# Adding each expert block straight into the output instead of summing the two expert results at the end

## The reference, cut to what matters

```python
xn = _layernorm(x, axis=-1)                       # x is 4096 x 256, float32
x = x + attention_and_ffn(xn) + experts(xn)

# experts(xf): 8 experts, 2 per token, F = 816
scores = softmax(xf @ gate_w.T + gate_b)
top_w, top_idx = top_k(scores, 2)
top_w = top_w / (top_w.sum(-1, keepdims=True) + 1e-20)
comb = zeros((N, E)).at[arange(N)[:, None], top_idx].add(top_w)
for e in range(E):
    h = silu((xf @ gp_w[e].T + gp_b[e]) * (xf @ up_w[e].T + up_b[e]))
    y += comb[:, e:e+1] * (h @ down_w[e].T + down_b[e])
```

## Time and profile before

| | us |
|---|---|
| median of 3 runs (lowest to highest) | 1273.86 (1269.78 to 1274.48) |
| the profiled execution | 1273.59 |
| its span, first to last instruction | 1271.7 |
| PE busy | 1119.9 (88%) |
| DVE busy | 880.4 (69%) |
| ACT busy | 852.1 (67%) |
| POOL busy | 633.3 (50%) |

### The profile page before, as it was taken

How to read it: one execution, slowest core, us unless ns; L and a number is a source line. 1 busy time by engine, 2 the same in 40 slices (tenths; PEclk the granted TensorE clock), 3 DMA queues, 4 the chain that set the end, 5 groups by cost and what they waited for, 6 DMA issues and landing times.

```text
span 1271.7 us, 29969 instructions
## 1 busy us (share of the span) xinstructions
PE 1119.9 (88%) x9148; PEld 1038.1 (82%) x9148; DVE 880.4 (69%) x2032; ACT 852.1 (67%) x1994; POOL 633.3 (50%) x912
## 2 busy tenths in 40 slices
PE   3978898989897979888999999999999989999950
PEld 3966686868686868777889999999999989999950
DVE  7467564747465655656678888888888888788825
ACT  2355766758585857586478887777787878887830
POOL 6003543233232314052167777777677767777750
PEclk9997898989898999999889999999999999999985
DMA  8870011010101010031241111114411240125119
GB/s 293 271 223 22 34 35 51 21 45 25 41 29 37 33 37 33 26 130 35 103 145 39 33 33 33 33 60 175 162 60 33 86 144 28 41 86 197 44 52 345
DMA packets 66258, 106.72 MB, mean 84 GB/s; under 512 B 7277, under 2 KB 57966, under 8 KB 64560
## 3 DMA queue, kind: packets, MB, share of 16 engines
q1 hardware_dynamic: 58624, 86.55, 20.9%
q0 software_dynamic: 7600, 19.74, 4.4%
HBM read 138.52 MB, written 37.50 MB: 138 GB/s over the span
## 4 chain that ended last, share of the span: by engine, by line
PE 36%; ACT 26%; DVE 19%; issue 13%; DMA 2%; SPq 1%; DVEq 1%; ACTq 1%; POOL 0%; POOLq 0%
PE bank L1198 9%; PE bank L1199 8%; PE bank L1200 8%; ACT hf L786 5%; DVE gu_s L1117 5%; ACT sm L689 4%; ACT gu_s L797 3%; ACT dw_s L804 3%; ACT gs L779 3%; DVE hf L1137 3%; PE bank L1295 3%; DVE gu_s L1124 3%; PE bank L1323 2%; DVE ys L1153 2%; PE bank L1285 2%
## 5 line engine op out<-in xcount | busy, mean ns | idle before, releaser
L1198 PE MATMUL bank<-xt_h,gu_s 128*128 128x256 f32 (+1 forms) x1014 | 294.8, 291 | 16.1 <-DVE hf L1137 11.3
L1199 PE MATMUL bank<-xt_l,gu_s 128*128 128x256 f32 (+1 forms) x1014 | 288.7, 285 | 0.0
L1200 PE MATMUL bank<-xt_h,gu_s 128*128 128x256 f32 (+1 forms) x1014 | 288.1, 284 | 0.0
L616 POOL TENSOR_TENSOR ht<-hf,ht 128x256 fp32r<-128x256 f32 (+1 forms) x273 | 240.2, 892 | 48.1 <-ACT ht L790 47.0
L1124 DVE TENSOR_TENSOR gu_s<-raw_gu,gu_s 128x512 fp32r<-128x512 f32 (+1 forms) x273 | 196.9, 744 | 64.0 <-ACT gu_s L797 63.9
L1198 PEld LDWEIGHTS bank<-xt_h,gu_s 128*128 128x128 f32 (+1 forms) x1014 | 193.5, 191 | 23.0 <-issue 19.8
L1200 PEld LDWEIGHTS bank<-xt_h,gu_s 128*128 128x128 f32 (+1 forms) x1014 | 193.5, 191 | 0.0
L1199 PEld LDWEIGHTS bank<-xt_l,gu_s 128*128 128x128 f32 (+1 forms) x1014 | 193.3, 191 | 0.0
L786 ACT ACTIVATE hf<-hf 128x256 f32<-128x256 f32 (+1 forms) x273 | 113.5, 416 | 77.0 <-DVE hf L1137 72.3
L1198 PE MATMUL bank<-dw_s,ht 128*128 128x256 f32 x546 | 154.8, 284 | 2.2 <-issue 2.2
L1200 PE MATMUL bank<-dw_s,ht 128*128 128x256 f32 x546 | 154.8, 283 | 0.0
(11 more groups left out here) (176 smaller groups left out, 2748.1 us busy)
## 6 DMA issues: line engine op xcount, KB each, us to landing
raw_gu<-in_gu_dram SPq DMA_DIRECT2D x39, 1648.0 KB
raw_dw<-in_dw_dram SPq DMA_DIRECT2D x39, 896.0 KB
xs_dram<-zrec SPq DMA_DIRECT2D x6, 1677.0 KB, 14.6
xr<-xs_dram SPq DMA_DIRECT2D x39, 258.0 KB, 2.7
yg<-y_dram SPq DMA_DIRECT2D x16, 512.0 KB, 8.3
xwin<-xn_dram SPq DMA_DIRECT2D x8, 640.0 KB, 4.8
xg<-in_x_dram SPq DMA_DIRECT2D x8, 512.0 KB, 6.3
xn_dram<-xg SPq DMA_DIRECT2D x8, 512.0 KB, 7.9
```

The source lines that it names most:

```text
L616: nc.gpsimd.tensor_tensor(ht[0:m, p, 1, c, :], hf[0:m, ring(c), :], ht[0:m, p, 0, c, :].bitcast(F32), ALU.subtract).then_inc(h_split, 1)
L1198: nc.tensor.matmul(dst, lhs[0], rhs[0], start=start, stop=False)
L1199: nc.tensor.matmul(dst, lhs[0], rhs[1], start=False, stop=False)
L1200: return nc.tensor.matmul(dst, lhs[1], rhs[0], start=False, stop=stop)
```

## The change

Three things change. The dense sums are stored to `out` by SP as soon as they are ready, seven groups in the dense stage and the last one in the beginning of the expert stage. For each expert block POOL gathers the block's rows of `out` with two indirect DMAs (`rows_so_far`) into `sofar`, which lies in the first four row tiles of `xn`; DVE adds them while it weighs, and the scatter goes to `out`. The last pass (`load_rows`, `add_rows`, the stores) is gone, and so is `y_dram`. POOL waits for all eight stores and clears `sofar` once before its first block.

```diff
@@ SP
+            def store_out(g):
+                sp.dma_start(out_g[ds(g, 1)].rearrange("o p t d -> p (o t) d"), xn[:, ds(g * GT, GT), :]).then_inc(out_stored, 16)
...
                 load_residual(at.g)
+                store_out(at.f)
...
             load_gu(2, 0)
             load_dw(1, 1, False)
+            store_out(NG - 1)
             load_rows_of(2, 0)
...
             sp.wait_ge(y_sent[0], 32 * ((NB + 1) // 2))
             sp.wait_ge(y_sent[1], 32 * (NB // 2))
-            (load_rows, store_out and their loop over the eight groups)
@@ POOL
+            def rows_so_far(b, p):
+                if not isinstance(b, int) or b >= 1:
+                    pool.wait_ge(y_sent[1 - p], (b + p) * 16)
+                if not isinstance(b, int) or b >= 2:
+                    settle(pool)
+                    pool.wait_ge(y_sent[p], (b - p) * 16)
+                pool.wait_ge(y_kept, b * 2 + 2)
+                settle(pool)
+                for t in range(2):
+                    index = dest[:, 2 * p + t:2 * p + t + 1]
+                    nc.gpsimd.indirect_dma_start(sofar[:, p, t, :], None, out, bass.IndirectOffsetOnAxis(index, 0),
+                                                 bounds_check=S - 1, oob_is_err=False).then_inc(sofar_loaded[p], 16)
...
             def body(b, p):
                 for c in range(FCH):
                     h_low(b, p, c)
                     if c == 2:
                         keep_meta(b, p)
+                    if c == FCH - 1 and (not isinstance(b, int) or b >= 1):
+                        rows_so_far(b - 1, 1 - p)
                 for c in range(DV, FCH):
                     dw_low(b, p, c)
                 if not isinstance(b, int) or b >= 1:
                     send(b - 1, 1 - p)
+            pool.wait_ge(out_stored, 16 * NG)
+            nc.gpsimd.memset(xn[:, 0:4, :], 0.0).then_inc(sofar_set, 1)
+            pool.wait_ge(sofar_set, 1)
             blocks_of(pool, body)
+            rows_so_far(NB - 1, (NB - 1) % 2)
             send(NB - 1, (NB - 1) % 2)
@@ DVE, weigh
+                dve.wait_ge(sofar_loaded[p], through(b, p, 32))
                 for t in range(2):
-                    ins = nc.vector.tensor_scalar(ys[:, p, t, :], bank[5 + p][:, t * D:(t + 1) * D], wgt[:, p, t:t + 1], None, ALU.mult)
+                    ins = nc.vector.scalar_tensor_tensor(ys[:, p, t, :], bank[5 + p][:, t * D:(t + 1) * D], wgt[:, p, t:t + 1], sofar[:, p, t, :], ALU.mult, ALU.add)
...
-            (add_rows and its loop)
```

More of the change, by code:

```diff
@@ L20 @@
 GT = 4
-YB = 4
 XB = 4
@@ L137, in program @@
     xs_dram = nc.dram_tensor("xs_dram", (SLOTS, REC), F32, kind="Internal").ap()
-    y_dram = nc.dram_tensor("y_dram", (2 * S, D), F32, kind="Internal").ap()
     with ExitStack() as ctx:
@@ L232, in program @@
         ys = tile("ys", [2, 2, D])
+        sofar = xn[:, 0:4, :].rearrange("p (b t) d -> p b t d", t=2)
         dest = tile("dest", [4], U32)
@@ L235, in program @@
         third.close()
-        fourth, tile = phase()
-        yg = tile("yg", [YB, 2, GT, D])
-        fourth.close()
         const_loaded, small_loaded, zrec_ready, xs_filled, pads_filled = sems("const_loaded small_loaded zrec_ready xs_filled pads_filled")
@@ L266, in program @@
         y_sent = sems("y_sent_0 y_sent_1")
-        yg_loaded = sems("yg_loaded_0 yg_loaded_1 yg_loaded_2 yg_loaded_3")
-        sum_1, sum_2, out_stored = sems("sum_1 sum_2 out_stored")
+        out_stored, sofar_set = sems("out_stored sofar_set")
+        sofar_loaded = sems("sofar_loaded_0 sofar_loaded_1")
         x_g = x.rearrange("(g t p) d -> g p t d", t=GT, p=P)
@@ L490, in _ @@
             sp.wait_ge(y_sent[1], 32 * (NB // 2))
[L492 to L508, removed]
         @block.gpsimd
@@ L521, in _ @@
             pool.wait_ge(zrec_ready, 1)
-            nc.gpsimd.iota(zrec[:, D:D + 1].bitcast(I32), [[0, 1]], base=2 * S, channel_multiplier=1).then_inc(zrec_ready, 1)
+            nc.gpsimd.iota(zrec[:, D:D + 1].bitcast(I32), [[0, 1]], base=S, channel_multiplier=1).then_inc(zrec_ready, 1)
             for n, (_, dst, chunks, width) in enumerate(DENSE):
@@ L622, in send @@
                     index = dest[:, 2 * p + t:2 * p + t + 1]
-                    nc.gpsimd.indirect_dma_start(y_dram, bass.IndirectOffsetOnAxis(index, 0), ys[:, p, t, :], None,
-                                                 bounds_check=2 * S - 1, oob_is_err=False).then_inc(y_sent[p], 16)
+                    nc.gpsimd.indirect_dma_start(out, bass.IndirectOffsetOnAxis(index, 0), ys[:, p, t, :], None,
+                                                 bounds_check=S - 1, oob_is_err=False).then_inc(y_sent[p], 16)
             def body(b, p):
@@ L898, in route_weights @@
                 for k in range(2):
-                    link(nc.vector.tensor_scalar(meta[:, k, :, 0].bitcast(I32), cst[:, C_TOK:C_TOK + NT], float(k * S), None, ALU.add))
+                    link(nc.vector.tensor_copy(meta[:, k, :, 0].bitcast(I32), cst[:, C_TOK:C_TOK + NT]))
             def route_starts(at):
@@ L1180, in _ @@
             weigh(NB - 1, (NB - 1) % 2)
[L1183 to L1191, removed]
         @block.tensor
```

## The result

The changed kernel takes 1378.3 us (median of 4 runs, 1375.84 to 1380.22) against 1272.3 us before (4 runs, 1269.78 to 1274.48): a ratio of 1.083, 95% interval 1.080 to 1.086. It is slower, as forecast, but by 106 us where 24 were forecast, and far above the range. The profiled execution spans 1376.0 us (before 1271.7), so 104.3 us are to be explained.

What follows compares the result with a forecast made beforehand. DMA bound the last pass, PE the expert stage. Added 9 + 1.5 + 48 + 2.7 = 61.2 us, less 37.5 removed, net +23.7 on 1273.59, gave 1298 us; the 8-in-10 range was 1274 to 1326.

Steps and rivals of the forecast that it cites:

- The direction: Whole kernel: slower by net 23.7 us; the chance of slower in all was put at 0.78.
- The stores in the dense stage: Seven 512 KB stores on SP's queue, covered by PE's work: cost 0, about 10 us if the cover were gone.
- The first block: POOL's first h_low waits for the last store and the clearing, delaying DVE and PE: 9 us, bounds 5 and 12.
- the first gather: The gather of block 0 adds one more 1.5 us, outside the 36 steady periods.
- The landing after the second gather: In each block, 2.4 to 2.7 us from the second gather's start; weigh period 16.6 us instead of 15.09.
- Rival C: Slow gathers: 3.5 us landings in all blocks, 1338 us; or 2 us each in nine weight-load blocks, 1316; chance 0.13.
- The loads: Blocks with weight loads: of 8 us excess over 36 periods, 6 absorbed because scatters stand about 1.4 us earlier.
- The removed pass: Last pass, 37.8 us to the span's end, less about 0.3 of closing instructions: gain 37.5 us in full.
- the end: Last two blocks wait for their gathers; the last scatters land at 1236.5 against 1233.87: 2.7 us added.
- what POOL loses in idle time: POOL's extra gather work, 39 x 2.5 us, fits its idle time, being busy 443 of 614 us: cost 0.
- rival A: Gather short and mostly hidden in each block, 0.7 us a block: 1264 us; chance 0.10.
- Rival D: PE's clock falls once in five blocks for some 7 us, costing 14 us: 1312 us; chance 0.05.

Runs made afterwards that it cites:

- experiment 1: Changed kernel without the gathers; DVE weighs by a multiply alone, so the output lacks the dense part in gathered rows: 1250.3 us, ratio 0.979.
- experiment 4: Changed kernel with DVE's one 128x1024 subtraction (dw_low) cut in four of 128x256: 1336.6 us, ratio 1.047.
- Experiment 3: Changed kernel with one more wait on SP, so the gate/up weight load is issued only after POOL's dw_low of the same body: 1342.6 us, ratio 1.052.
- Experiment 2: Changed kernel with the gathers issued by POOL, but DVE neither waits for them nor adds them: 1298.7 us, ratio 1.017.
- experiment 5: Changed kernel with the two gathers moved on POOL from behind the last h_low to behind keep_meta, after its third h_low: 1338.7 us, ratio 1.049.
- e10: Changed kernel weighing block b-2 behind chunk 2 of body b, scatter behind the third h_low, last store awaited at the first gather: 1271.9 us, ratio 0.998.
- e6: Changed kernel without clearing the tile, POOL's wait for the last store moved from before the first block to before the first gather: 1371.6 us, ratio 1.074.
- e9: Changed kernel weighing block b-2 behind chunk 3 of body b, scatter behind the fourth h_low, last store awaited at the first gather: 1286.2 us, ratio 1.011.

## Why the prediction was wrong

**Right.** The direction, and what paces the stage: `weigh` waits for the second gather in every block and PE for the product behind it. The stores in the dense stage were free, as worked out. So was part of the account of the loads: POOL's wait for a slow scatter (15.0 us in 8 waits) is gone in the changed kernel. The first block's +10.3 us for 10.5 is in part luck: counted from the end of the dense stage in each profile, `weigh` 0 is 6.7 us late in experiment 1, without gathers (I took 9), and the first gather adds 2.9 (I took 1.5).

**The landing after the second gather was mis-sized** ("lands after 2.4 (what the second of a quiet pair takes)"). It is 3.6 to 3.7 us from the start of the issue, also 0.9 more than the 2.7 that I allowed at most. I read the scatters' row, whose second issue takes 1.00 us at a place where DVE is past its long operation. A gather issued where I put it begins within that operation, and experiment 4 shows that this alone costs 0.86 us. I had written that DVE "is still at its splits" there and still allowed only 0.3 us. The h_low end was 0.4 us earlier than I took, which gave a part back; net 0.68 us a block, 24.4 us in all. Rival C's first form (3.5 us in every block) had the landing nearly right.

**The loads were mis-sized, and with the wrong sign** ("I count 6 of the 8 us as absorbed"). I looked only at the wait that I knew, for the scatters, and not at where the new gather lies against SP's loads, though rival C says that they "start about 1 us behind the second gather and could overtake it". C gave it 2 us in nine blocks; these nine are 5.3 us longer each (47.6 us), 4.2 of it the wait for the gather. Experiment 3 shows it: 36 us come back by a later load alone; and in experiment 4 eight of the nine go by an issue that ends before the load starts. C's two forms together are what happened, and I had priced each on its own and never their sum: 40 + 18 us above 1298 is 1356, still 22 short.

**The removed pass was worth 34.5 us, not 37.5**, since the program's closing isn't 0.3 us; and the end costs 4.7 us for 2.7, since each of the last gathers also takes longer.

**What no rival had**: POOL's issues cost by themselves. I had put "what POOL loses in idle time" at 0, from its 443 busy us of 614. Experiment 2 puts the period at 16.2 with nothing waiting for the data. In the changed kernel the wait hides this floor (17.28), so the term isn't in the miss, but rival A (1264 us if the gather is hidden) could never have come true in this order of work; experiment 5, built on it, came 64 us above its range. Rival D's clock falls came (mean 0.94 where before it was 0.99): four quiet periods of 18.1 instead of 17.3 make 3 us, and up to some 10 us more lie in the load blocks, behind the idle that the collisions make. The latter is read from the lengths of the periods, and no run tests it apart.

What stays open: in experiment 1 the closing from the last `weigh` takes 10.8 us, and 8.3 to 8.4 in the changed kernel and all the others; and what sets e10's period.

## What to carry to other kernels

When a pass that runs alone at the DMA's rate is turned into one small transfer a block, compare it with the number of blocks times the slack of the engines that issue it and wait for it, and not with bytes: here 2.2 us more in each of 36 periods, and 5.3 on top in nine of them, outweighed 34.5 us of a pass that moved 12.6 MB. Price a new DMA from the operations of the neighbouring engine at its exact place and from the loads that start before its issue ends, in the blocks where there are any. Let what it fetches be wanted a third of a block later, not next.

## What the runs showed of the hardware

- An indirect DMA's issue on POOL takes 1.0 to 1.4 us nearly everywhere, unless it begins while a DVE operation with two inputs of 128x1024 f32 (1.23 us) runs. An issue that began 0.1 to 1.0 us into it ended 0.87 to 0.96 us behind its end, in the changed kernel and in e2, e3, e6 and e9: it took 2.06 us when begun 0.11 us into it, 1.88 at 0.24, 1.57 at 0.6. The 28 of e10 that began 0.1 to 0.2 us before it took 1.07 or 1.08. With the operation in pieces of 256 columns the issue took 1.02.
- It goes the other way as well: POOL's unbroken run of seven 128x256 two-input operations stretches three DVE operations of 128x512 from 1.72 to 5.04 us. The Trainium skill (GPSIMD Engine Reference, Specifications) says that POOL's interfaces to SBUF are shared with VectorE, with contention where a DVE instruction has two SBUF inputs. The traces agree, and give it these sizes.
- A gather of 0.13 MB that is still being issued (0.55 us to go) as a load of 1.7 MB starts lands 7.8 us after its start, about when the load is done. With the load 0.3 us behind the end of the issue (e4) it has landed within 3.5 us of its own start.
- Gathers whose rows are mostly padding (0.04 MB for a pair instead of 0.26 MB) let `weigh` go 0.6 us sooner: the idle time before it is 2.07 us at 1343.42 instead of 2.7.
